# Sums over states in quads: batching the column-tiled matmuls of a selective scan

## Chip, cores, metric

One NeuronCore of a Trainium2 chip runs the whole kernel. The metric is the device time of one execution in microseconds; for the kernel before it is the median of three timed runs.

## The reference, cut to what matters

Two blocks run one after the other on x of (16, 192, 32, 32); each adds its result to x. The first is a convolution with a chunked state-space scan (SSD). The second is a selective scan:

```
proj  = seq @ W_proj.T + b_proj              # seq: (B, 1024, 192)
x_in, delta, Bm, Cm = split(proj)            # 192, 192, 16, 16 columns
delta = softplus(delta + dt_bias)
h_t = exp(delta_t * A) * h_{t-1} + (delta_t * x_t) * B_t      # (192 channels, 16 states)
y_t = sum over the 16 states of h_t * C_t    # the sums over states
out = (y + x_in * D) @ W_out.T + b_out
x   = x + out
```

Everything is float32.

## The kernel before

**Units.** The scan of one image is cut into two halves of 512 positions, and each half into 24 units. A unit is one block of 32 channels (`BLK`) with one group of 4 states, so that it fills 128 partitions. The first 16 units of a half (`WIDE`) are the four wide blocks, channels 0 to 127, group by group: units 4g to 4g + 3 are the four blocks of group g. The other 8 are the two narrow blocks, channels 128 to 191, two to a group. `unit(i)` gives group and block.

**The life of unit i.** ACT makes the decay exp(delta A) (L936), DVE the input product (L1220) and the scan over 512 positions (L1233, `hst`, a ring of 3). POOL multiplies by C into `hc`, a ring of 6 (`CRING`, L747). PE sums over the 4 states by a matmul with `sel` (128 x 32): the output are 32 partitions of the bank B_YSUM, at 32 times the block for wide units, so that the blocks of a group use different column tiles of the array. All groups of a half accumulate in the bank; `sum_states` opens it with diag1a times x_in. After the last wide sum ACT copies the bank (`copy_wide`, L942), PE opens the rows of the narrow blocks again (`start_rest`, diag1b), and after the last narrow sum ACT copies them (`copy_rest`).

**The batches.** `sum_states(n, k)` sums BATCH = 2 units, for whose products it waits by the semaphore hc_ready. PE raises y_sum_ps once a batch, and POOL waits for it before it writes the slot that held unit i - 6:

```
if i >= CRING or prev:
    pool.wait_ge(y_sum_ps.sem, y_sum_ps.at(n, (i - CRING) // BATCH + 1))
```

**The slots.** Every engine runs its own instructions in a fixed order that is written out by slots s = 0 to 47. One pass of 48 slots scans image b and does, woven in, the first block of image b + 1: fills (s = 0 to 2), four convolutions on PE (s = 3, 5, 7, 10) whose results ACT copies one slot later, eight chunks that start at s = 13, 15, ..., 27 and whose stages follow until s = 36, then the group means and variances of the result (s = 37, 38), and from s = 40 the projection of the second block. The output of the scan's first half (identity, wo1a and wo1b products, `finish`) is at s = 37 to 40, that of the second at s = 10 to 13 of the next pass. In slot s the scan is at unit s - 1 on DVE and at unit s - 2 on POOL. PE takes the batches at every even slot: units i, i + 1 (i even) at s = i + 4, first thing in the slot. The batches of units 44 to 47 fall into s = 0 and 2 of the next pass. There are 17 passes; 15 have both a scan and a first block, the one before them has no scan, the last no first block.

Line 1282 is that of the helper `mm`, which issues nearly all matmuls; L1366, L1380, L1381 and L1428 issue the rest. A float32 matmul is two instructions.

Of the kernel before, what the change touches and what calls it, by code (L numbers as in the profile page):

```python
# [49 lines left out]
NG = S1 // SG  # L50
NB = C // BLK
WB = P // BLK
HALF = L // 2
CPH = HALF // Q
HU = NG * NB
UNITS = 2 * HU
# [47 lines left out]
SLOTS_DU, DRING, WRING, HRING, CRING = 4, 3, 2, 3, 6  # L104
LEAD = 3


BATCH = 2
BATCHES = UNITS // BATCH
HALF_BATCHES = HU // BATCH  # L110
WIDE = NG * WB
WIDE_BATCHES = WIDE // BATCH


def unit(i):
# [56 lines left out]
def build(nc, scratch, x_d, inw_d, cw_d, cb_d, dtb_d, alog0_d, d0_d, nw_d, nb_d, outw_d,  # L172
          wp_d, bp_d, alog1_d, d1_d, dtb1_d, wo_d, bo_d, out_d):
    with ExitStack() as ctx:  # L174
# [209 lines left out]
        hc_ready = sig("hc_ready", UNITS)  # L384
        y_sum_ps = sig("y_sum_ps", BATCHES)
        y1_copied = sig("y1_copied", 4)
# [40 lines left out]
        for r in range(7):  # L427
            n = min(P, PROJ0 - r * P)
# [6 lines left out]
        for r in range(2):  # L435
            n = P if r == 0 else CB_
            for m in range(XM):
                jobs.append((nato[0:n, r, m * P:(m + 1) * P], n, P, [(wo0[:, m, r * P:r * P + n], 0, n)]))
        for r in range(4):
            n = min(P, PROJ1 - r * P)  # L440
# [10 lines left out]
        for r in range(2):  # L451
            n = P if r == 0 else CB_
# [196 lines left out]
        def _(pool):  # L649
# [86 lines left out]
            def states_by_c(n, i, prev):  # L736

                hf, (g, k) = i // HU, unit(i)
                pool.wait_ge(scanned.sem, scanned.at(n, i + 1))
                if k == 0:  # L740
                    pool.wait_ge(bc_read[g].sem, bc_read[g].at(n, 16 * (hf + 1)))
                if i == last_of_group(0, 0):

                    pool.wait_ge(kept_bc.sem, kept_bc.at(n, 16 * 4))
                if i >= CRING or prev:
                    pool.wait_ge(y_sum_ps.sem, y_sum_ps.at(n, (i - CRING) // BATCH + 1))  # L746
                nc.gpsimd.tensor_tensor(hc[:, i % CRING, :], hst[:, i % HRING, :], bcrep[:, g, 1, :],  # L747
                                        ALU.mult).then_inc(hc_ready.sem, 1)

# [18 lines left out]
        def _(act):  # L768
# [170 lines left out]
            def copy_wide(n, hf):  # L939

                act.wait_ge(y_sum_ps.sem, y_sum_ps.at(n, HALF_BATCHES * hf + WIDE_BATCHES))
                nc.scalar.copy(y1a[:, :], bank[B_YSUM][:, :]).then_inc(y1_copied.sem, 1)  # L942

            def copy_rest(n, hf):

                r = slice(hf * CB_, (hf + 1) * CB_)
                act.wait_ge(y_sum_ps.sem, y_sum_ps.at(n, HALF_BATCHES * (hf + 1)))
                nc.scalar.copy(y1b[r, :], bank[B_YSUM][r, :]).then_inc(y1_copied.sem, 1)
# [14 lines left out]
            def run(b, par, scan, end, first, more):  # L963
                step = Steps(act, act_steps, b + 1)
                mid_step = Steps(act, act_mid_steps, b)
                for s in range(SLOTS if scan or first else END_AT[1] + END_STEPS):
                    if scan:

                        decay(b, s, end, first)
                    if scan:  # L970
                        second_half(b, s, par, mid_step)
                    if first:
                        first_block(b + 1, s, step, 1 - par, scan, end)
                    if scan:
                        if 2 <= s < HU + 2:
                            act.wait_ge(scanned.sem, scanned.at(b, s - 1))
                            nc.scalar.copy(carry[:, s - 2:s - 1], hst[:, (s - 2) % HRING, HALF - 1:HALF]).then_inc(carried.sem, 1)  # L977
                        for hf in range(2):
                            if s == hf * HU + BATCH * WIDE_BATCHES + 2:
                                copy_wide(b, hf)  # L980
                        if s == HU + 2:
                            copy_rest(b, 0)
                    if end:
                        if s == 2:
                            copy_rest(b - 1, 1)
                        finish(b - 1, s, 1, 1 - par)
                    if scan:
                        finish(b, s, 0, par)
                assert not first or step.done == ACT_STEPS, step.done
# [281 lines left out]
        def _(pe):  # L1271
# [258 lines left out]
            def sum_states(n, k, prev):  # L1530

                hf, kk = k // HALF_BATCHES, k % HALF_BATCHES
                if kk == 0:
                    if hf or prev:
                        pe.wait_ge(y1_copied.sem, y1_copied.at(n, 2 * hf))
                    pe.wait_ge(p1_copied.sem, p1_copied.at(n, (K_XA, K_X2)[hf]))
                    mm(bank[B_YSUM][:, :], diag1a[:, :], xcm[:, PIECE[hf], :], True, False)
                pe.wait_ge(hc_ready.sem, hc_ready.at(n, BATCH * (k + 1)))
                for i in range(BATCH * k, BATCH * (k + 1)):
                    g, blk = unit(i)  # L1540
                    r0 = BLK * blk if blk < WB else hf * CB_ + BLK * (blk - WB)
                    ins = mm(bank[B_YSUM][r0:r0 + BLK, :], sel[:, :], hc[:, i % CRING, :], False, g == NG - 1)
                ins.then_inc(y_sum_ps.sem, 1)
# [20 lines left out]

            def run(b, par, scan, end, first, more):
                for s in range(SLOTS if scan or first else END_AT[1] + END_STEPS):
                    if s in (0, BATCH):
                        if end:
                            sum_states(b - 1, BATCHES - 2 + s // BATCH, False)
                    elif scan and s > 2 and (s - 2) % BATCH == 0:  # L1570
                        sum_states(b, (s - 2) // BATCH - 1, end)
                    for hf in range(2):
                        if scan and s == hf * HU + WIDE + 3:
                            start_rest(b, hf)
                    if end:
                        if scan and s == END_AT[1]:

                            pe.wait_ge(scanned.sem, scanned.at(b, 8))
                        if not scan and s == END_AT[1]:

                            pe.wait_ge(scanned.sem, scanned.at(b - 1, UNITS))
                        finish(b - 1, s, 1, 1 - par)
                        if s == SSD_AT + 5:

                            pe.wait_ge(out_ready.sem, out_ready.at(b - 1, 4))
                    if scan:
                        if first and s == END_AT[0]:

                            pe.wait_ge(row_exp.sem, row_exp.at(b + 1, NRB * NCH))
                        if s == END_AT[0]:  # L1590
                            pe.wait_ge(scanned.sem, scanned.at(b, 36))
                        finish(b, s, 0, par)
                    if first:
                        first_block(b + 1, s, end if scan else None)
                    if more and s == EARLY_AT + 1:
                        pe.wait_ge(p1_copied.sem, p1_copied.at(b + 1, 2))
                        group_means(b + 2, 0)
                    if more and s == EARLY_AT + 2:
                        group_variances(b + 2, 0)
# [47 lines left out]
```

## Time and profile before

| | |
|---|---|
| timed runs | 3646.38, 3640.47, 3628.37 us; median 3640.47 |
| the profiled execution | 3614.94 us, span 3613.2 us |
| mean granted TensorE clock | 0.929 |
| PE busy | 3140.8 us (87%) |
| weight loads (PEld) | 1812.4 us (50%) |
| DVE busy | 2674.8 us (74%) |
| ACT busy | 1840.2 us (51%) |
| POOL busy | 1507.1 us (42%) |
| POOL waits for DVE before L747 | 1143.3 us |
| PE waits for POOL's hc | 101.4 us |

A busy PE means that a matmul is in flight, not that the array is full. The granted clock is 1.00 at 2.4 GHz and 0.50 at 1.2 GHz. Times in rows are microseconds from the start of the span. In a timeline row stand the start, the duration, the engine and line, output and inputs, how many instructions are merged in it, and in brackets the idle time of the engine before it with what ended it.

### The profile page before, as it was taken

The page shows a single profiled execution, that of the slowest core. Times are in us where ns is not written, and L with a number is a line of the kernel's source. Part 1 is how long each engine was busy: PE and PEld are TensorE (multiplying, and loading weights), DVE is VectorE, ACT ScalarE, POOL GpSimd, SP SyncE. Part 2 cuts the span into 40 slices and gives each one's busy share as a digit, 9 for nine tenths or more (in the row PEclk, how much of TensorE's full clock was granted, in tenths as well). Part 3 has the DMA queues.
Part 4 walks back from the last instruction along what each step waited for, and adds up shares of the span by engine and source line. Part 5 has one row for each costly group of instructions (what it writes and reads, how often), then busy time and mean ns, then how long its engine had stood idle before and what let it go on. Part 6 is the DMA issues. An engine that isn't in the chain of part 4 may idle for free. (4 is left out here: it accounts for less than half of the span.)

```text
span 3613.2 us, 60645 instructions
## 1 busy us (share of the span) xinstructions
PE 3140.8 (87%) x20256; PEld 1812.4 (50%) x20256; DVE 2674.8 (74%) x3983; ACT 1840.2 (51%) x4315; POOL 1507.1 (42%) x1107
## 2 busy tenths in 40 slices
PE   4888889898899998889898898998899999888965
PEld 2655547364463735547364453735446364554710
DVE  1347877778677777878778787777868778787787
ACT  1536464554636446364553646446464554646432
POOL 1014444444444344444444444344434444444455
PEclk8999999998989989999998999999989998999976
DMA  2032141413214142141412314141231413214121
GB/s 58 14 103 64 39 137 36 132 68 93 85 45 123 56 123 71 38 134 38 131 68 85 91 44 131 50 131 68 70 101 45 117 68 105 79 47 133 36 99 65
DMA packets 104163, 290.96 MB, mean 81 GB/s; under 512 B 25373, under 2 KB 27020, under 8 KB 103820
## 3 DMA queue, kind: packets, MB, share of 16 engines
q1 hardware_dynamic: 103820, 286.71, 26.3%
q8 instruction: 176, 2.88, 0.3%
q14 instruction: 167, 1.37, 0.1%
HBM read 181.84 MB, written 39.85 MB: 61 GB/s over the span
## 5 line engine op out<-in xcount | busy, mean ns | idle before, releaser
L747 POOL TENSOR_TENSOR hc<-hst,bcrep 128x512 f32<-128x512 f32 x768 | 1202.5, 1566 | 1178.4 <-DVE hst L1233 1143.3
L833 ACT ACTIVATE ssd<-bank,ncs 128x128 f32<-128x128 f32 x1536 | 438.8, 384 | 237.2 <-PE bank L1282 237.0
L1282 PE MATMUL bank<-hc,sel 128*32 128x512 f32 x1536 | 454.3, 677 | 101.4 <-POOL hc L747 101.4
L1220 DVE TENSOR_TENSOR wr<-durep,bcrep 128x512 f32<-128x512 f32 x768 | 521.1, 679 | 3.6 <-DMA bcrep<-bc_rows 3.6
L1233 DVE TENSOR_TENSOR_SCAN hst<-dec,wr 128x512 f32<-128x512 f32 x256 | 392.4, 1533 | 92.5 <-ACT carry L977 58.5
L1282 PE MATMUL bank<-ssd 128*128 128x32 f32 (+1 forms) x3296 | 447.2, 288 | 0.0
L936 ACT ACTIVATE bank<-durep,aneg 128x512 f32<-128x512 f32 x368 | 253.9, 690 | 294.1 <-DVE hst L1233 285.5
L1282 PEld LDWEIGHTS bank<-ssd 128*128 128x128 f32 x3296 | 399.5, 193 | 4.2
L1282 PE MATMUL bank<-ssd,wcv 64*32 64x512 f32 x5376 | 349.7, 600 | 0.0
L1282 PE MATMUL bank<-xna,wt0a 128*128 128x128 f32 (+3 forms) x1088 | 296.1, 374 | 34.1 <-DVE xnb L1044 34.1
L866 ACT ACTIVATE ssd<-bank,nbc,nwc 128x128 f32<-128x128 f32 x384 | 147.5, 453 | 345.8 <-PE bank L1428 345.8
L1233 DVE TENSOR_TENSOR_SCAN hst<-bank,carry,wr 128x512 f32<-128x512 f32 x240 | 306.2, 1276 | 11.2 <-ACT bank L936 1.9
L936 ACT ACTIVATE dec<-durep,aneg 128x512 f32<-128x512 f32 x400 | 292.8, 738 | 6.7 <-DVE hst L1233 4.7
L714 POOL TENSOR_TENSOR lrs<-lve,neghalf 128x1 f32<-128x1 f32 x128 | 87.1, 680 | 484.4 <-DVE lve L1087 484.4
L1282 PE MATMUL bank<-xnb,wt0b 128*128 128x128 f32 (+3 forms) x1088 | 285.2, 364 | 0.0
L1081 DVE TENSOR_TENSOR ssd<-ssd,bank 128x384 f32<-128x384 f32 x112 | 62.1, 554 | 283.7 <-PE bank L1282 283.7
L1366 PE MATMUL bank<-ident,csum 128*128 128x128 f32 x1536 | 239.5, 280 | 17.7 <-ACT ssd L833 12.6
L708 POOL TENSOR_TENSOR ssd<-ssd,wend 128x384 f32<-128x384 f32 x112 | 144.0, 1286 | 248.6 <-ACT ssd L879 248.6
L1282 PE MATMUL bank<-ssd,wo 128*128 128x128 f32 (+1 forms) x1536 | 212.6, 280 | 33.4 <-DVE x1b L1112 33.3
L1282 PEld LDWEIGHTS bank<-xna,wt0a 128*128 128x128 f32 (+1 forms) x1088 | 174.2, 194 | 134.4 <-issue 86.4
L1099 DVE TENSOR_TENSOR ssd<-ssd,bank 128x1536 f32<-128x1536 f32 x128 | 223.4, 1746 | 23.1 <-ACT ssd L833 23.1
L1366 PEld LDWEIGHTS bank<-ident,csum 128*128 128x128 f32 x1536 | 184.6, 141 | 87.7 <-issue 41.7
(187 smaller groups left out, 5000.8 us busy)
## 6 DMA issues: line engine op xcount, KB each, us to landing
durep<-scratch SPq DMA_DIRECT2D x192, 512.0 KB, 3.7
bcrep<-bc_rows SPq DMA_DIRECT2D x128, 512.0 KB, 5.2
ssd<-stage SPq DMA_DIRECT2D x384, 140.4 KB, 2.9
ssd<-bcst SPq DMA_DIRECT2D x128, 74.4 KB, 2.7
xa<-in_x_dram SPq DMA_DIRECT2D x16, 512.0 KB, 4.0
scratch<-u SPq DMA_DIRECT2D x32, 256.0 KB, 2.1
scratch<-delta SPq DMA_DIRECT2D x32, 256.0 KB, 2.4
out_dram<-x1a SPq DMA_DIRECT2D x16, 512.0 KB, 4.8
```

Of the source, the lines that this page charges most:

```text
L708: nc.gpsimd.tensor_tensor(xw[:, c % 2, :].rearrange("p (h d) -> p h d", d=HD), xtok[:, c % 2, 0:DI].rearrange("p (h d) -> p h d", d=HD), b ...
L714: nc.gpsimd.tensor_tensor(lrs[:, c % 2:c % 2 + 1], lve[:, c % 2:c % 2 + 1], neghalf[:, 0:1], ALU.pow).then_inc(lrs_ready.sem, 1)
L747: nc.gpsimd.tensor_tensor(hc[:, i % CRING, :], hst[:, i % HRING, :], bcrep[:, g, 1, :], ALU.mult).then_inc(hc_ready.sem, 1)
L833: ins = nc.scalar.activation(att[:, c % 2, h, :], bank[ROW_BANKS[r]][:, k * Q:(k + 1) * Q], ACT.Exp, bias=ncs[:, c, h:h + 1])
L866: ins = nc.scalar.activation(yzt[:, c % 2, m, :], bank[B_CBT][:, (m + 1) * Q:(m + 2) * Q], ACT.Identity, bias=nbc[:, m:m + 1], scale=nwc[: ...
L936: nc.scalar.activation(decay_of(i), durep[:, j % SLOTS_DU, 0, :], ACT.Exp, scale=aneg1[:, g * NB + k:g * NB + k + 1]).then_inc(decay_ready ...
L1081: ins = nc.vector.tensor_tensor(y0[:, c % 2, :], yint[:, c % 2, :], bank[B_XY][:, 0:DI], ALU.add)
L1099: nc.vector.tensor_tensor(a, a, bc(bank[B_CBT][:, 0:Q].unsqueeze(1), [P, NH, Q]), ALU.mult).then_inc(att_ready.sem, 1)
L1220: nc.vector.tensor_tensor(wr[:, i % WRING, :], durep[:, j % SLOTS_DU, 1, :], bcrep[:, g, 0, :], ALU.mult).then_inc(w_made.sem, 1)
L1233: nc.vector.tensor_tensor_scan(hst[:, i % HRING, :], decay_of(i), wr[:, i % WRING, :], carry[:, g:g + 1] if hf else 0.0, ALU.mult, ALU.add ...
L1282: return nc.tensor.matmul(out, lhsT, rhs, start=start, stop=stop, skip_group_check=True)
L1366: nc.tensor.matmul(ps[:, k * Q:(k + 1) * Q], bc(csum[:, 0, c, h:h + 1], [P, P]), ident[:, :], start=(k == 0), stop=False, is_transpose=Tru ...
```

## The change

The wide units are now summed four at a time, which are the four blocks of a group, and the narrow ones two at a time as before. The quads stand at s = 6, 10, 14, 18 and s = 30, 34, 38, 42; there are 8 batches in a half instead of 12. A quad is due when its last unit is, which is where the second of its two pairs was; the first pair of each four moves there, two slots later. The product with diag1a moves with the first batch of a half, from s = 4 to 6 and from s = 28 to 30. POOL's wait for a ring slot counts the new batches. ACT's `copy_wide` stays at its slots.

```diff
-BATCH = 2
-BATCHES = UNITS // BATCH
-HALF_BATCHES = HU // BATCH
 WIDE = NG * WB
-WIDE_BATCHES = WIDE // BATCH
+BATCH_SIZES = (WB,) * NG + (NB - WB,) * NG
+HALF_BATCHES = len(BATCH_SIZES)
+BATCHES = 2 * HALF_BATCHES
+WIDE_BATCHES = NG
+BATCH_END = [hf * HU + sum(BATCH_SIZES[:k + 1]) for hf in range(2) for k in range(HALF_BATCHES)]
+
+
+def batch_of(i):
+
+    return min(k for k in range(BATCHES) if i < BATCH_END[k])
...
                 if i >= CRING or prev:
-                    pool.wait_ge(y_sum_ps.sem, y_sum_ps.at(n, (i - CRING) // BATCH + 1))
+                    pool.wait_ge(y_sum_ps.sem, y_sum_ps.at(n, batch_of(i - CRING) + 1 if i >= CRING else batch_of(i - CRING + UNITS) + 1 - BATCHES))
...
-                            if s == hf * HU + BATCH * WIDE_BATCHES + 2:
+                            if s == hf * HU + WIDE + 2:
                                 copy_wide(b, hf)
...
-                pe.wait_ge(hc_ready.sem, hc_ready.at(n, BATCH * (k + 1)))
-                for i in range(BATCH * k, BATCH * (k + 1)):
+                pe.wait_ge(hc_ready.sem, hc_ready.at(n, BATCH_END[k]))
+                for i in range(BATCH_END[k] - BATCH_SIZES[kk], BATCH_END[k]):
...
-                    if s in (0, BATCH):
-                        if end:
-                            sum_states(b - 1, BATCHES - 2 + s // BATCH, False)
-                    elif scan and s > 2 and (s - 2) % BATCH == 0:
-                        sum_states(b, (s - 2) // BATCH - 1, end)
+                    for k in range(BATCHES):
+                        if end and s + UNITS == BATCH_END[k] + 2:
+                            sum_states(b - 1, k, False)
+                        if scan and s == BATCH_END[k] + 2:
+                            sum_states(b, k, end)
```

## Rows read from the trace of the kernel before

**Rows 1.** the page, part 5: the sums over states (count, busy together, mean ns of one)
```profile
L1282 PE MATMUL bank<-hc,sel 128*32 128x512 f32 x1536 | 454.3, 677 | 101.4 <-POOL hc L747 101.4
```

**Rows 2.** busy times by pass, three of 14 and the sum; granted clock behind POOL
```profile
1320.40:1542.20 221.80, 198.83 (x1264) 114.96 (x1264) 166.46 (x248) 114.00 (x267) 93.19 (x68) 0.92 0.27 82
1542.20:1754.10 211.90, 190.51 (x1264) 110.13 (x1264) 165.69 (x248) 114.58 (x268) 90.64 (x67) 0.96 0.28 86
...
2610.40:2835.90 225.50, 203.42 (x1264) 117.01 (x1264) 165.70 (x248) 113.59 (x266) 92.34 (x68) 0.90 0.27 81
...
sum 3014.30, PE 2707.05 PEld 1571.47 DVE 2320.80 ACT 1597.03 POOL 1297.24; mean PE 193.36 PEld 112.25 DVE 165.77 ACT 114.07 POOL 92.66
```

**Rows 3.** timeline of PE, s = 28 to 33 (start, us, what; idle before)
```profile
1682.27 1.02 PE L1282 MATMUL bank<-xcm,diag1a 128*128 128x512 f32 x2
1683.23 1.05 PE L1282 MATMUL bank<-hc,sel 128*32 128x512 f32 x4
1684.21 0.91 PE L1282 MATMUL bank<-state,cs_ 128*128 128x384 f32 x2
...
1703.43 0.55 PE L1428 MATMUL bank<-ident,ssd 128*128 128x128 f32 x3 [0.82 <-DVE ssd L1091]
```

**Rows 4.** timeline of DVE, where it waits for PE
```profile
1509.59 0.16 DVE L1039 TENSOR_SCALAR gv<-bank 128x2 f32<-128x2 f32 x1 [4.08 <-PE bank L1282]
...
1689.08 0.55 DVE L1081 TENSOR_TENSOR ssd<-ssd,bank 128x384 f32<-128x384 f32 x1 [2.40 <-PE bank L1282]
...
1725.11 0.80 DVE L1044 TENSOR_SCALAR xnb<-x1b,gm,gr 64x1024 f32<-64x1024 f32 x1
...
1733.43 0.43 DVE L1049 TENSOR_SCALAR u<-ssd 128x512 f32<-128x512 f32 x1 [1.83 <-ACT ssd L913]
```

**Rows 5.** timeline of PE, s = 4 to 17
```profile
1568.35 1.13 PE L1282 MATMUL bank<-xcm,diag1a 128*128 128x512 f32 x2
...
1583.05 1.05 PE L1282 MATMUL bank<-hc,sel 128*32 128x512 f32 x4
1586.80 1.05 PE L1282 MATMUL bank<-hc,sel 128*32 128x512 f32 x4 [2.70 <-POOL hc L747]
...
1610.33 0.91 PE L1282 MATMUL bank<-state,cs_ 128*128 128x384 f32 x2 [2.11 <-DVE state L1059]
```

**Rows 6.** timeline of ACT before the last convolution's copies, in two passes
```profile
1375.11 0.68 ACT L796 ACTIVATE xs<-bank,cb 64x512 f32<-64x512 f32 x1 [2.72 <-PE bank L1282]
...
1594.44 0.68 ACT L796 ACTIVATE xs<-bank,cb 64x512 f32<-64x512 f32 x1 [1.07 <-PE bank L1282]
```

**Rows 7.** timeline of PE, a pair beside a projection onto 32 columns
```profile
1539.19 1.07 PE L1282 MATMUL bank<-hc,sel 128*32 128x512 f32 x2
1539.20 1.06 PE L1282 MATMUL bank<-xna,wt1a 128*32 128x512 f32 x1
```

**Rows 8.** timeline of PE, s = 37 to 40
```profile
1714.02 1.83 PE L1282 MATMUL bank<-x1a,ident 128*128 128x512 f32 x2
1716.22 0.38 PE L1282 MATMUL bank<-mv,ga 128*128 128x1 f32 x2 [0.38 <-DVE mv L1028]
...
1722.70 1.92 PE L1282 MATMUL bank<-hc,sel 128*32 128x512 f32 x4 [0.36 <-POOL hc L747]
...
1727.11 1.12 PE L1282 MATMUL bank<-xna,wt1a 128*128 128x512 f32 x2
```

**Rows 9.** granted clock (behind POOL) behind gaps of PE, in short stretches
```profile
1367.50:1370.50 3.00, 3.00 (x28) 1.18 (x34) 0.70 (x1) 2.97 (x8) 1.04 (x1) 0.50 0.00 0
...
1500.50:1514.00 13.50, 13.50 (x30) 5.03 (x31) 9.11 (x13) 1.96 (x3) 5.42 (x4) 0.50 0.37 126
1589.30:1592.30 3.00, 3.00 (x64) 1.09 (x56) 1.52 (x2) 2.97 (x8) 0.46 (x2) 1.00 0.02 5
...
3515.00:3570.00 55.00, 24.31 (x48) 2.85 (x48) 53.10 (x43) 17.84 (x35) 33.96 (x22) 0.50 0.30 100
```

**Rows 10.** timeline of PE in the last pass, one pair of many alike
```profile
3532.40 1.92 PE L1282 MATMUL bank<-hc,sel 128*32 128x512 f32 x4 [3.65 <-POOL hc L747]
```

## The prediction, made before the change was run

> **What bounds the kernel now.** I read the page first, then the busy times by pass, then one pass (1542.2 to 1754.1) engine by engine as a timeline, and last the stretches where the granted clock is low. A pass does a scan of one image (48 units of 512 positions, two halves of 24: 16 units of the wide blocks, then 8 of the narrow) and the first block of the next image, woven together by slots s = 0 to 47; 15 of the 17 passes do both. The sums over states are 1536 PE instructions, but they overlap: 454 us busy together for 1040 us of single durations [rows 1]. A pass takes 215.3 us in the mean over the 14 that I measured; the three shown take 211.9 to 225.5, and what differs between them is the clock: 0.96 in the shortest, 0.92 and 0.90 in the longer ones [rows 2]. So there are two kinds of limit: places where PE is the last to arrive, and places where PE is early but comes back from a gap at half clock.
>
> PE is the last to arrive in the chunk part (s = 20 to 31): it has nearly no gap, and DVE waits for it, 2.40 us before chunk 6 at 1689.08 [rows 3, 4]. After the last chunk DVE is the limit for most of the time, then PE's projection is (DVE waits 1.83 us at 1733.43 through ACT's softplus) [rows 4]. In s = 4 to 17 ACT and DVE set the time, with one exception: ACT waits 1.07 us for the last convolution, which PE began late because its sum at s = 10 waited 2.70 us for POOL [rows 5, 6].
>
> **The change part by part.** The order before is a pair at every even slot; after, the wide units have a quad at s = 6, 10, 14, 18 and at s = 30, 34, 38, 42. So the pairs at s = 4, 8, 12, 16, 28, 32, 36 and 40 go, the diag1a product that opens each half moves with its first batch (4 to 6, 28 to 30), and the pairs of the narrow units stay. No DMA is added or moved; instructions are as many as before.
>
> A quad's price: a pair takes 0.98 us from start to start (1683.23 to 1684.21) at full clock [rows 3]. No quad is in the trace. From above it can't cost more than two pairs, 1.96; from below not less than a pair. The nearest row is three column tiles at once: at 1539.19 two of hc and, 0.01 us later, one of the projection onto 32 columns start together, and take 1.07 and 1.06 us as tiles of a pair do at that clock [rows 7]. I take 0.98 for a quad. The Trainium skill (TensorE: Matmul & The Clock Gate, Measured speedup vs the span model) gives 3.07 times for four row tiles, not 4; by that a quad would be near 1.1 us, and 8 quads would give back about 1 us a pass if all lay on the path.
>
> *s = 28 and 30.* Before: diag1a 0.96 + pair 0.98 at s = 28, pair 0.98 at s = 30. After: nothing, then 0.96 + 0.98. The first chunk output comes 1.94 earlier, which DVE's wait of 2.40 allows; by the next, net gain 1.94 - 0.96 = 0.98. With up to 0.15 for a dearer quad I take 0.88. PE is gap-free in between, so it goes to the end of the pass.
>
> *s = 40.* In the pass shown PE waits 0.36 for POOL, then the pair takes 1.92 at half clock (from 1722.70), and the projection starts at 1727.11. It needs DVE's xnb, done at 1725.91 (1725.11 + 0.80) [rows 4, 8]. Without the pair PE is there first, so the gain is 1727.11 - 1725.91 = 1.2 us, and DVE's wait of 1.83 leaves room for it. Bounds: 0 and 1.83.
>
> *s = 32, 36.* The next PE work waits for DVE: 0.82 us at 1703.43 and 0.38 at 1716.22 [rows 3, 8]. No gain. *s = 4, 8, 12, 16.* At 4 and 8 PE is ahead (2.70 of gap follows), at 12 ACT is the limit, at 16 the gap of 2.11 at 1610.33 follows [rows 5]. No gain.
>
> Gain, with the clock as it is: 15 passes x (0.88 + 1.2) = 31 us.
>
> *What the empty places cost.* The hidden pairs were what kept PE's gaps short.
> First, s = 7 to 10. The convolution now ends 1.94 - 0.96 = 0.98 earlier and the pair at 1583.05 is gone, while the sum at s = 10 still waits for unit 7 at 1586.80, which hangs on DVE and ACT. The gap of 2.70 becomes 1586.80 - 1582.07 = 4.7 us. Behind it are quad, identity product and the convolution for which ACT waits. What a low clock costs there is in the trace: in the pass from 1320.4 the clock was at its lower level, 1.2 GHz (0.50 from 1367.5 on), after the same gap of 2.70, and ACT waited 2.72 instead of 1.07 us: 1.65 us [rows 6, 9]. In the pass from 1542.2 it stayed at 1.00. Low after this gap: 4 of the 14 passes, counted in the same way. The last pass shows what longer gaps do: with 3.65 us between pairs PE ran at 0.50 for all of 3515 to 3570 [rows 9, 10]. I take it that after 4.7 us it is always low, and for longer (up to 3.3, two such stretches; nothing if it stays high): 2.2 us in about 10 passes more, 22 us.
> The Trainium skill (same page, HAM oscillation) says that idle PE between bursts drops the clock each time; if so, all passes pay here, and the trace agrees for gaps of 3.65 us, while after 2.70 it goes both ways.
> Second, s = 17: the gap of 2.11 [rows 5] becomes 3.1, before from_state and chunk 0, for which DVE waits. Low there in 3 of 14 passes; I take half: 5 more x 1.65 = 8 us (0 to 20).
> Third, s = 36 to 38. The identity product (1714.02) follows a pair that took 1.9 us at half clock; without it, it starts at 1712.1 and at full clock ends by 1713.1; then nothing until 1716.22 [rows 8]: a gap of 3.1 us. Behind it lie the group sums, the quad, four output products and the group variance, which DVE needs. In the pass from 1320.4 the clock was 0.50 from 1500.5 to 1514.0, and DVE waited 4.08 us for the variance (1509.59); in the pass from 1542.2 not at all [rows 4, 9]. Long low stretches are in 5 of 14 passes. I take 12 of 15: 7 more x 4.1 = 29 us (0 to 41).
>
> Sum: -31 + 22 + 8 + 29 = +28 us. The profiled execution took 3614.94 us (span 3613.2), so 3643 in its terms. The three timed runs have a median of 3640.47, 25.5 above it; the profile's own passes differ by up to 13.6 us (225.5 - 211.9) through the clock, so I read these 25 us as more passes with a low clock. A part of the loss is then already in the median. I count 12 of the 28 instead: 3652.
>
> **The rivals.**
> A, *the clock stays as it was.* The gaps grow but the clock falls no more often than now; only the 31 us remain: 3640 - 31 = 3609. For it: after 2.70 us the clock stayed up in 10 of 14 passes, and total PE work is no less dense. Against: 4.7 us is longer than any gap in these 14 passes. It decides if the clock is at 1.00 behind the sum at s = 10 in more than half of the passes.
> B, *the forecast*: gains eaten by half-clock stretches, 3652.
> C, *heavier*: the low stretch behind s = 10 lasts over the whole convolution (3.3 us a pass) and the one at s = 36 comes in every pass: 15 x (2.1 - 3.3 - 1.65 x 0.5) + the third at 41 gives about 71 of loss less what is paid already (25): 3686.
> D, *the four tiles don't run together*: a quad costs 1.96. Then s = 28 and 30 gain 0, s = 40 keeps its 18 us, and the gaps still cost 59: 3640 + 41, less the 16 already paid: 3665. Against it: three tiles at once in the trace.
> E, *POOL waits for its ring.* hc has 6 slots, and units 4m and 4m + 1 come free two slots later than before. POOL needs them two slots behind the quad. If each wait lasted a quad: 8 x 0.98 x 16 = 125 us, 3765. Against: the pairs before were four slots ahead, and half of that is left.
>
> **How the numbers follow.** A 0.30, B 0.48, C 0.14, D 0.05, E 0.03. B's own range is 3635 to 3675. The range over all that holds 8 in 10 goes from A's 3605 to 3686. A change of 0.5% (18 us) is about what a measurement can tell from none: faster means under 3622, slower over 3659. Faster: A and a trace of B, 0.31. Same: most of B, 0.35. Slower: the rest of B with C, D, E, 0.34.
>
> **What would show it.** A quad's eight instructions spanning about 1.05 us at full clock (D wrong). Chunks 5 to 6 closer by about 2 us, 6 to 7 farther by about 1 us. PE idle 4.7 us before the sum at s = 10 and the clock 0.50 behind it; ACT's wait for the last convolution over 2.7 us. DVE's wait of about 4 us for the variance in most passes. Mean clock down from 0.929 to about 0.90. A mean clock of 0.93 or more would make B wrong and A right; POOL waits for PE above today's would speak for E.

## The result: 0.7% slower

After, five runs: 3661.28 to 3669.55 us, median 3666.45. Before, in five runs beside them: 3628.37 to 3646.38, median 3642.82. The ratio after to before is 1.0068, 95% interval 1.0045 to 1.0091. So the change costs about 24 us, more than the 0.5% that can be told from none. In the later comparisons, with 16 to 27 runs, the kernel before had medians of 3627 to 3634 and single runs from 3596 to 3661: its time varies from run to run more than that of the kernel after, whose five runs lie within 8.3 us.

The profiled execution after took 3669.55 us (span 3667.8), mean granted clock 0.904. Before it was 3614.94 (3613.2) and 0.929. The profiles are thus 54.6 us apart where the medians are 24: the profiled run of before was one of its quick ones. Where the time went is read from the profiles, how much it is from the medians.

The page of the kernel after, part 1 (busy time of PE to POOL) and the group of part 5 that stands in [rows 1]:
```profile
PE 3101.3 (85%) x20256; PEld 1839.3 (50%) x20256; DVE 2677.0 (73%) x3983; ACT 1841.4 (50%) x4315; POOL 1519.0 (41%) x1107
...
L1288 PE MATMUL bank<-hc,sel 128*32 128x512 f32 x1536 | 317.0, 713 | 135.1 <-POOL hc L753 135.1
```
The change did what it says. The same 1536 instructions are busy together for 317 us instead of 454, and PE for 3101 instead of 3141. DVE, ACT and POOL have the same work. The mean of one sum rose from 677 to 713 ns, although nothing in it changed: 366 of the 1536 now start in a stretch at half clock, before 252. (Lines from L753 on stand 6 further down than before.)

Busy times by pass of the kernel after, as in [rows 2] (granted clock behind POOL), three of 14 and their sum:
```profile
1339.00:1560.60 221.60, 194.17 (x1266) 115.51 (x1264) 166.61 (x248) 113.99 (x267) 93.91 (x68) 0.91 0.27 82
1560.60:1779.30 218.70, 191.71 (x1264) 114.47 (x1264) 165.92 (x248) 114.37 (x268) 91.67 (x67) 0.91 0.27 82
...
2656.50:2878.20 221.70, 194.21 (x1264) 115.40 (x1264) 165.98 (x249) 113.99 (x268) 94.39 (x68) 0.91 0.27 82
...
sum 3067.30, PE 2679.16 PEld 1596.45 DVE 2323.18 ACT 1597.64 POOL 1309.56; mean PE 191.37 PEld 114.03 DVE 165.94 ACT 114.12 POOL 93.54
```
A pass takes 219.1 us (3067.3 / 14) instead of 215.3. Before, 7 of the 14 took 209.3 to 211.9 and the others up to 225.5. Now all but the first take 218.2 to 221.7, at a clock of 0.91 to 0.92: the quick passes are gone, and so are the slowest.

To find the place I cut each pass at events of DVE and ACT that stand in the same order in both kernels, and took the mean over the 14 passes of each trace. The cuts: DVE's first write of xna (start), ACT's last copy of a convolution, DVE's first statistics instruction (lst) behind the outputs of chunks 0, 1, 5, 6 and 7, its read of the group variance (gv), its product u of delta and x. Worked out from starts in the traces, us:

```
                 conv.  chunk 0  0-1    1-5    5-6    6-7    gv     u      end   pass
before           55.69  19.54   11.96  49.03  13.46   9.42  23.83  19.40  12.97  215.3
after            57.41  20.84   12.89  49.03  11.42  10.48  24.16  19.74  13.13  219.1
difference       +1.72  +1.30   +0.93   0     -2.04  +1.06  +0.33  +0.34  +0.16   +3.8
```
Times 14 (unrounded) this is 53.1; what stands ahead of the 14 passes is 5.1 longer and what stands behind them 3.6 shorter, which makes the 54.6 by which the spans differ.

**The places themselves.** Timeline of PE after, s = 6 to 18 and 36 to 37, in the pass that is the counterpart of [rows 5]:
```profile
1592.36 1.13 PE L1288 MATMUL bank<-xcm,diag1a 128*128 128x512 f32 x2
1593.41 1.06 PE L1288 MATMUL bank<-hc,sel 128*32 128x512 f32 x8
1594.41 0.46 PE L1288 MATMUL bank<-da,upper 128*128 128x96 f32 x2
...
1605.20 1.94 PE L1288 MATMUL bank<-hc,sel 128*32 128x512 f32 x8 [4.65 <-POOL hc L753]
1607.07 2.08 PE L1288 MATMUL bank<-x1a,ident 128*128 128x512 f32 x2
...
1631.39 1.65 PE L1288 MATMUL bank<-state,cs_ 128*128 128x384 f32 x2 [3.09 <-DVE state L1065]
...
1644.41 1.13 PE L1288 MATMUL bank<-state,cs_ 128*128 128x384 f32 x2 [2.96 <-DVE state L1068]
...
1733.81 1.74 PE L1288 MATMUL bank<-ssd,wo 128*128 128x128 f32 x12 [1.06 <-DVE x1b L1118]
1736.96 1.13 PE L1288 MATMUL bank<-x1a,ident 128*128 128x512 f32 x2 [1.41 <-DVE hst L1239]
1739.56 0.38 PE L1288 MATMUL bank<-mv,ga 128*128 128x1 f32 x2 [1.47 <-DVE mv L1034]
```
A quad costs 1.00 us from start to start (1593.41 to 1594.41) at full clock and 1.87 at half (1605.20 to 1607.07). The first two gaps are the ones that the forecast worked out: 4.7 and 3.1 us. The one of 2.96 us behind them was as long before. The forecast's third gap, 3.1 us ahead of the group sums (mv,ga), is not there: the identity product waits for DVE's scan and splits it into 1.41 and 1.47 us.

Who waits behind them, ACT and DVE in the same pass ([rows 4, 6]):
```profile
1615.51 0.68 ACT L802 ACTIVATE xs<-bank,cb 64x512 f32<-64x512 f32 x1 [3.74 <-PE bank L1288]
```
```profile
1637.85 0.56 DVE L1084 COPY ssd<-bank 128x384 f32<-128x384 f32 x1 [4.22 <-PE bank L1288]
1650.90 0.55 DVE L1087 TENSOR_TENSOR ssd<-ssd,bank 128x384 f32<-128x384 f32 x1 [4.07 <-PE bank L1288]
...
1699.93 0.56 DVE L1087 TENSOR_TENSOR ssd<-ssd,bank 128x384 f32<-128x384 f32 x1 [2.77 <-PE bank L1288]
1711.35 0.56 DVE L1087 TENSOR_TENSOR ssd<-ssd,bank 128x384 f32<-128x384 f32 x1 [0.35 <-PE bank L1288]
1721.84 0.56 DVE L1087 TENSOR_TENSOR ssd<-ssd,bank 128x384 f32<-128x384 f32 x1 [2.26 <-PE bank L1288]
...
1735.62 1.28 DVE L1239 TENSOR_TENSOR_SCAN hst<-bank,carry,wr 128x512 f32<-128x512 f32 x1
...
1746.33 0.16 DVE L1045 TENSOR_SCALAR gv<-bank 128x2 f32<-128x2 f32 x1 [1.46 <-PE bank L1288]
```
ACT waits 3.74 us where it waited 1.07 (or 2.72 in the pass with a low clock there). Before chunk 6 DVE's wait of 2.40 has shrunk to 0.35: the gain at s = 28 is there.

Busy times in short stretches of that pass, granted clock behind POOL, as in [rows 9]:
```profile
1604.00:1607.00 3.00, 1.80 (x8) 0.20 (x8) 2.72 (x3) 2.92 (x6) 1.84 (x2) 0.50 0.00 0
1607.00:1610.00 3.00, 3.00 (x16) 1.40 (x20) 0.82 (x1) 2.99 (x7) 0.93 (x1) 0.50 0.00 0
...
1631.50:1634.50 3.00, 3.00 (x9) 2.13 (x10) 2.11 (x3) 0.14 (x1) 1.63 (x1) 0.50 0.21 81
1645.00:1648.00 3.00, 3.00 (x14) 2.52 (x12) 1.83 (x3) 1.14 (x4) 1.49 (x1) 0.50 0.00 0
...
1740.50:1743.80 3.30, 3.30 (x11) 0.72 (x11) 3.09 (x7) 0.00 (x0) 1.63 (x1) 0.50 0.80 264
1743.90:1747.20 3.30, 3.30 (x13) 1.45 (x12) 1.73 (x4) 1.27 (x2) 2.26 (x2) 1.00 0.48 150
1747.30:1754.00 6.70, 6.65 (x8) 1.75 (x8) 6.61 (x8) 2.07 (x3) 3.18 (x2) 0.50 0.01 6
```
A low stretch is a stretch of time at half clock. In 14 of 14 passes one begins behind s = 10 (before in 4), in 13 and 13 behind the gaps ahead of the first two products with a state (before in 3 and 5), which the outputs of chunks 0 and 1 follow. The third stretch stands at s = 37 to 40, and the last three rows show it from s = 38 on: it is broken up, low behind the gap, high, low again into the projection at s = 40.

### The profile page after: what moved, and what is told of

Same layout as the page of the kernel before. It is cut to its first block and busy times, and to the rows that moved or that the text cites. A ratio compares the mean times of both kernels' runs of the same rounds, so it can differ in the third digit from the quotient of the medians.

```text
span 3667.8 us, 60519 instructions
## 1 busy us (share of the span) xinstructions
PE 3101.3 (85%) x20256; PEld 1839.3 (50%) x20256; DVE 2677.0 (73%) x3983; ACT 1841.4 (50%) x4315; POOL 1519.0 (41%) x1107
## 5 line engine op out<-in xcount | busy, mean ns | idle before, releaser
L753 POOL TENSOR_TENSOR hc<-hst,bcrep 128x512 f32<-128x512 f32 x768 | 1213.8, 1581 | 1205.0 <-DVE hst L1239 1154.5
L1288 PE MATMUL bank<-hc,sel 128*32 128x512 f32 x1536 | 317.0, 713 | 135.1 <-POOL hc L753 135.1
L1372 PE MATMUL bank<-ident,csum 128*128 128x128 f32 x1536 | 250.0, 289 | 32.5 <-ACT ssd L839 26.4
L1372 PEld LDWEIGHTS bank<-ident,csum 128*128 128x128 f32 x1536 | 193.2, 146 | 108.0 <-issue 50.1
L1288 PE MATMUL bank<-ssd,wo 128*128 128x128 f32 (+1 forms) x1536 | 212.3, 281 | 26.3 <-DVE x1b L1118 26.3
```

Of the source, the lines that this page charges most:

```text
L1288: return nc.tensor.matmul(out, lhsT, rhs, start=start, stop=stop, skip_group_check=True)
L1372: nc.tensor.matmul(ps[:, k * Q:(k + 1) * Q], bc(csum[:, 0, c, h:h + 1], [P, P]), ident[:, :], start=(k == 0), stop=False, is_transpose=Tru ...
```

## The experiments

"Dummy pairs" are products with a tile of zeros, added to the open bank, so that the result doesn't change; each pair is four instructions, as dear as a pair of hc. The edit is the same in all kernels that have them, and only the table differs:

```diff
+            def keep_busy(s):
+                where, pairs = KEEP_BUSY.get(s, (None, 0))
+                for _ in range(pairs):
+                    for r0 in (0, BLK):
+                        mm(bank[where][r0:r0 + BLK, :], nosel[:, :], wt0a[:, 0:HALF], where != B_YSUM, where != B_YSUM)
...
+                    if scan and first and s != 18:
+                        keep_busy(s)
```
At s = 18 they go to another bank, since ACT reads the sums then. The last pass has none. Theory 1 is the forecast's: PE's idle time, and the half clock behind it, is the cost of the change.

**First set: parts of the change, and less work.** Beside these four the kernel before had a median of 3634.01.

*e1_fill_back*, from the kernel after:
```diff
+KEEP_BUSY = {8: (2, 2), 16: (2, 1), 36: (2, 1)}
```


> Changed kernel plus dummy products (zero weights, 128 x 32, added to the open bank, so nothing changes in the result) in the places of the removed pairs ahead of PE's gaps: two pairs at s = 8, one at s = 16, one at s = 36. PE's gaps are then about as long as before the change, and nothing else differs from the changed kernel. Theory (the clock falls behind longer gaps): the gain of 31 us shows, 3600 to 3630 us; clock 0.92 or more. Rival (the quads or POOL's ring waits cost the time): adding 4 pairs of work a pass can't help, 3666 us or more. Rival (the clock falls whatever one does): 3660 to 3670.

Measured: 3664.14, ratio 1.0087 (1.0053 to 1.0122), in the range of the last rival and not of the theory.

*e2_quads_first_half* and *e3_quads_second_half* have quads in one half of the image only:
```diff
-BATCH_SIZES = (WB,) * NG + (NB - WB,) * NG
+SIZES = ((WB,) * NG + (NB - WB,) * NG, (2,) * (HU // 2))     # e2
+SIZES = ((2,) * (HU // 2), (WB,) * NG + (NB - WB,) * NG)     # e3
```


> Quads in the first half only (s = 6 to 18), pairs in the second half. Theory: this part has the costs (gaps before the sums at s = 10 and before s = 17) and no gain: 3665 to 3700 us, slower than both. Rival (quads cost by themselves, evenly): half of the change's 24 us, about 3655.

> Quads in the second half only (s = 30 to 42), pairs in the first. Theory: this part has both gains (0.9 us at s = 28 and 30, 1.2 us at s = 40, in 15 passes) and only the third gap: 3600 to 3630 us, faster than before. Rival (quads cost by themselves): about 3655.

Measured: e2 3722.28, ratio 1.0248 (1.0208 to 1.0289); e3 3667.57, ratio 1.0101 (1.0067 to 1.0134).

*e4_less_work* is the kernel before with pairs everywhere, where the sums of units 4, 5, 12 and 13 of the first half take only the first of their 512 columns (this part of the sums is left out):
```diff
+                    w = 1 if i in THIN else HALF
-                    ins = mm(bank[B_YSUM][r0:r0 + BLK, :], sel[:, :], hc[:, i % CRING, :], False, g == NG - 1)
+                    ins = mm(bank[B_YSUM][r0:r0 + BLK, 0:w], sel[:, :], hc[:, i % CRING, 0:w], False, g == NG - 1)
```


> Kernel before, but the pairs of units 4, 5 (s = 8) and 12, 13 (s = 16) sum only 1 of their 512 columns; that part of the sum is left out. PE does nearly 2 us of work less a pass, and no wait or order changes. Theory: the gaps before s = 10 and s = 17 grow to 3.6 and 3.0 us, the clock falls behind them more often, and the kernel is slower with less work: 3655 to 3690 us. Rival (a pair in PE's idle time costs nothing, leaving it out changes nothing): 3635 to 3648.

Measured: 3733.83, ratio 1.0268 (1.0228 to 1.0308), clock 0.898. PE timeline of this kernel, the rows with a gap at the three places:
```profile
1624.80 1.92 PE L1288 MATMUL bank<-hc,sel 128*32 128x512 f32 x4 [3.55 <-POOL hc L753]
...
1651.01 1.65 PE L1288 MATMUL bank<-state,cs_ 128*128 128x384 f32 x2 [2.92 <-DVE state L1065]
1664.02 1.13 PE L1288 MATMUL bank<-state,cs_ 128*128 128x384 f32 x2 [2.97 <-DVE state L1068]
```
This is the clearest run of the four. Two pairs all but gone in front of two gaps, nothing moved and no quad, and the kernel is 100 us slower, far beyond what was expected. The clock is low at the same three places as in the kernel after (14, 13 and 14 of 14 passes). About half of the 8.8 us a pass falls at the third stretch (gv and u in the table below, 2.8 and 1.8), whose gaps the edit doesn't touch: the clock is low there for 13.6 to 20.5 us in all 14 passes, before in 5. The run speaks against any theory in which the quads' order or their price is the cost.

The other three missed too: e2 is 22 us over the upper end of what was expected, and e1 and e3, expected at 3600 to 3630, are as slow as the kernel after. With the same cuts as above:

```
                 conv.  chunk 0  0-1    1-5    5-6    6-7    gv     u      end   pass
e1 fill back     55.48  20.06   13.47  49.75  11.42  10.49  24.73  20.51  12.51  218.4
e2 first half    57.66  20.65   13.02  49.03  13.45   9.41  25.38  19.76  12.57  220.9
e3 second half   56.00  19.91   13.33  49.66  11.42  10.49  24.70  20.56  12.87  218.9
e4 less work     57.57  20.70   13.02  49.04  13.46   9.42  26.62  21.15  13.14  224.1
```
Quads in the second half alone bring the gain between chunks 5 and 7 and leave the gap at s = 10 as it was (2.73 us), though the clock is low behind it in 7 passes instead of 4. But there the clock is low for longer ahead of chunk 1, behind a gap that is the same in all these kernels (12 passes of 14, before 5), and in the third stretch in all passes. The halves aren't additive either: 5.6 and 3.6 us a pass alone, 3.8 together. So a part of the change moves low stretches to gaps that it leaves alone. Theory 1 had to say what happens when no gap is left.

**Second set: fill more.** The kernel before had a median of 3627.21 here.

*e5_dummy_pairs_at_old_places*, from the kernel after, a pair at each place that lost one but s = 4 and 28:
```diff
+KEEP_BUSY = {8: (2, 1), 12: (2, 1), 16: (2, 1), 32: (2, 1), 36: (2, 1), 40: (2, 1)}
```


> The kernel after, with a dummy pair (four products of a zero weight tile, 128x32 by 128x512 each, as dear as a pair of hc) behind s = 8, 12, 16, 32, 36 and 40, where the kernel before has pairs; only s = 4 and 28 stay without. Results are not changed by it, PE's work is more than before's. Theory 1 (PE's idle time and the clock that follows from it make the loss): every gap is as long as in the kernel before, so the time is before's less the gain at s = 28 and 30, 15 x 0.95 = 14 us: 3610 to 3640, ratio to before 0.993 to 1.001. Rival (the quads themselves, by the order in which hc and the bank come free, or dummy work that delays PE): no better than the kernel after, 3660 or more.

Measured: 3656.99, ratio 1.0091 (1.0056 to 1.0126): a miss. PE timeline at s = 8 to 10:
```profile
1585.44 1.05 PE L1290 MATMUL bank<-wt0a,nosel 128*32 128x512 f32 x4
1590.17 1.94 PE L1290 MATMUL bank<-hc,sel 128*32 128x512 f32 x8 [3.68 <-POOL hc L755]
```
The expectation said that every gap is as long as before. It isn't: the convolution still ends 0.98 us earlier, because the pair of s = 4 isn't there, and the gap is 2.70 + 0.98 = 3.68. The clock is low behind it in all 14 passes, and the first cut is at 58.75. The third stretch, with the old pairs back at s = 32, 36 and 40, is near that of before (24.26 and 18.94).

*e6_one_quad*, only units 24 to 27 as a quad at s = 30:
```diff
+SIZES = ((2,) * (HU // 2), (WB,) + (2,) * 10)
```


> Only units 24 to 27 are summed as a quad, at s = 30; all other units go in pairs as before. So only the pair at s = 28 is gone, with its diag1a product moved to s = 30. Theory 1: the gain of 0.95 us a pass at s = 28 and 30 is there and no gap grows, 3640 - 14 = 3620 to 3630, ratio 0.996. Rival (the clock hits passes by their position, and any shift of a microsecond decides in how many of them a stretch goes low): anything from 3610 to 3670, with the low stretches of before in other passes.

Measured: 3638.5, ratio 1.003 (0.9997 to 1.0064), no difference that can be told from none. The 0.97 us gain between chunks 5 and 7 is there (11.42 + 10.49 against 13.46 + 9.42), and it is lost: low behind the unchanged gap ahead of chunk 1 in 10 passes instead of 5, gv 24.77 instead of 23.83. The rival, that any shift of a pass changes where the clock falls, fits better than theory 1 here.

*e7_before_filled*, the kernel before (pairs in both halves), with its own gaps filled, and *e8_after_filled*, the kernel after with all gaps over a microsecond filled but those at the pass's seam:
```diff
+KEEP_BUSY = {8: (2, 2), 16: (2, 1), 18: (0, 2), 35: (2, 1), 37: (2, 1)}                                  # e7
+KEEP_BUSY = {8: (2, 4), 16: (2, 2), 18: (0, 2), 32: (2, 1), 35: (2, 1), 36: (2, 2), 40: (2, 1)}      # e8
```


> The kernel before with dummy pairs of zero weights in its own gaps: two behind s = 8, one at s = 16, two at s = 18, one at s = 35 and one at s = 37; results are not changed. Theory 1: the gaps of 2.70, 2.11, 2.96 and those around s = 36 fall under 1.5 us, so the low stretches at 46, 70, 84 and 180 us of a pass come less often; with none of them all passes take the 211.5 of the fast ones or less, 16 x 3.8 = 60 us under the mean of after and 15 x 2 to 4 under this kernel's median: 3580 to 3615. Rival (filling moves the low stretches but doesn't take them away, as in the first experiment; the dummy pairs cost where they overlap with real work): 3630 to 3670.

> The kernel after with dummy pairs in all its gaps of over a microsecond: four behind s = 8, two at s = 16, two at s = 18, one at s = 32 and s = 35, two at s = 36, one at s = 40; results are not changed. Theory 1: no gap over 1.5 us is left but that at a pass's start, the low stretches at 43, 70, 84 and 180 us of a pass vanish, and each of their costs as measured in the trace of after (2.7, 2.1, 1.6 and 1.0 us) comes back, with the gain at s = 28 and 30 on top: a pass of 211 or less, 3570 to 3610. Rival (some of the low stretches stay, at other places): 3620 to 3670. If the dummy work only delays: over 3670.

Measured: e7 3579.04, ratio 0.9879 (0.9838 to 0.9920); e8 3563.38, ratio 0.9824 (0.9786 to 0.9863). Both are faster than both kernels, by doing more work; e7 is 1 us and e8 7 us under the lower end of what was expected. PE timeline of e8, s = 8 to 10 in one pass, then s = 18 in another:
```profile
1779.64 3.63 PE L1290 MATMUL bank<-wt0a,nosel 128*32 128x512 f32 x16
1784.38 1.06 PE L1290 MATMUL bank<-hc,sel 128*32 128x512 f32 x8 [1.11 <-POOL hc L755]
...
1786.55 5.38 PE L1290 MATMUL bank<-ssd,wcv 64*32 64x512 f32 x96
```
```profile
1601.26 1.89 PE L1290 MATMUL bank<-wt0a,nosel 128*32 128x512 f32 x8
1604.32 0.91 PE L1290 MATMUL bank<-state,cs_ 128*128 128x384 f32 x2 [1.17 <-DVE state L1070]
```
Busy times of e8 at the former low stretches (granted clock behind POOL), and its page:
```profile
1562.00:1582.00 20.00, 18.84 (x190) 5.33 (x174) 15.74 (x16) 18.62 (x32) 11.27 (x7) 1.00 0.00 1
1590.00:1610.00 20.00, 17.58 (x124) 12.45 (x120) 14.60 (x23) 9.10 (x30) 8.46 (x7) 1.00 0.33 108
1690.00:1705.00 15.00, 13.05 (x66) 5.27 (x60) 14.56 (x26) 4.17 (x7) 9.36 (x8) 1.00 0.31 106
1705.00:1718.00 13.00, 11.18 (x30) 3.10 (x31) 12.02 (x16) 6.81 (x12) 6.20 (x4) 1.00 0.05 21
```
```profile
L1290 PE MATMUL bank<-hc,sel 128*32 128x512 f32 x1536 | 292.2, 643 | 85.2 <-POOL hc L755 85.2
```
What waits still waits as long (PE's real work comes at the same time), but it finds the clock at 1.00. From the second of the 14 passes on there is no low stretch between 35 and 198 us of a pass. The same quads now take 643 ns each, not 713.

e8 is 16 us under e7 (not compared with each other in one ratio; both against the same runs of before). I had expected this from the gain of 0.97 us a pass at s = 28. The passes don't bear that out: they take 212.7 and 212.8, because e8 gives the gain back at the seam, where its convolutions end later (57.81 against 56.07): the clock is low in the first 40 us of a pass for 10.5 us in the mean, in e7 for 6.6. In the profiles e8 is 9.1 shorter, 8.3 of it in the last pass.

**Third set: one group of gaps opened again.** Each kernel is e8 without some of its dummy pairs. The kernel before had a median of 3632.6.
```diff
+KEEP_BUSY = {16: (2, 2), 18: (0, 2), 32: (2, 1), 35: (2, 1), 36: (2, 2), 40: (2, 1)}               # e9
+KEEP_BUSY = {8: (2, 4), 32: (2, 1), 35: (2, 1), 36: (2, 2), 40: (2, 1)}                            # e10
+KEEP_BUSY = {8: (2, 4), 16: (2, 2), 18: (0, 2)}                                                    # e11
+KEEP_BUSY = {44: (2, 2), 47: (2, 2), 8: (2, 4), 16: (2, 2), 18: (0, 2), 32: (2, 1), 35: (2, 1), 36: (2, 2), 40: (2, 1)}   # e12
```
In e12 those of s = 44 and 47 go to the rows of the narrow blocks, which are open then, and at s = 44 they stand behind the slot's projection.

> The kernel after with all the dummy pairs of the eighth experiment but the four behind s = 8, so that the gap of about 4.7 us before the quad at s = 10 is open again. Theory 1 (a gap brings half clock behind it and that is the cost, each gap for itself): the clock is 0.50 for about 7 us behind s = 10 in nearly every pass and the last convolution comes 2.7 us later, 15 x 2.7 = 40 us: 3595 to 3610 beside 3563. Rival (the costs aren't separate: the low stretch shifts the pass against the others, and what was filled stays filled, or later gaps get shorter by it): under 3580 if the delay is absorbed, over 3625 if other stretches fall too.

> The same without the dummy pairs at s = 16 and s = 18, so that the gaps of about 3.1 and 3.0 us before the first two state products are open. Theory 1: low stretches of 3.4 us at 70 and 84 us of a pass in most passes, for which DVE waits: 2.1 + 1.6 us a pass as in the trace of after, 15 x 3.7 = 55 us: 3600 to 3625. Rival: these gaps go low only when the one at s = 10 has gone low before (in the kernel before they fell in few passes); then under 3580.

> The same without the dummy pairs at s = 32, 35, 36 and 40. Theory 1, with the size as measured in after: low stretches around 180 us of a pass, 1.0 us a pass to the group variance and 1 more to the end by the projection at half clock: 3575 to 3600. With the size of the forecast, 4.1 us a pass: 3620 to 3630.

> All the dummy pairs of the eighth experiment and two more pairs at s = 44, ahead of the second group variance of the image after next (gap of 2.5 us), and two at s = 47, ahead of the next pass's first product (gap of 2.0 to 4.7 us). Results are not changed. Theory 1: the low stretches at 0 to 24 us of a pass (10 to 17 us in most passes) get rarer; before that the first products of a pass came up to 3.5 us later than in passes without: 3520 to 3560. Rival (what follows there waits for DVE or for loads, or the many products of 12 columns bring the low clock by themselves): 3560 to 3570, or over 3570 if the pairs delay the projection.

Measured: e9 3607.46, ratio 0.9925 (0.9892 to 0.9958); e10 3618.01, 0.9963 (0.9933 to 0.9992); e11 3614.39, 0.9963 (0.9932 to 0.9994); e12 3557.7, 0.9776 (0.9733 to 0.9819).

The rows that decide, of e9, e10 and e11: the instruction behind the gap in the timeline (in e11 DVE's read of the variance), and the granted clock of the stretch:
```profile
1576.48 1.93 PE L1290 MATMUL bank<-hc,sel 128*32 128x512 f32 x8 [4.67 <-POOL hc L755]
...
1575.60:1582.30 6.70, 5.82 (x33) 1.85 (x41) 4.29 (x4) 6.60 (x12) 2.98 (x3) 0.51 0.00 0
1590.00:1640.00 50.00, 45.06 (x297) 31.39 (x298) 39.23 (x57) 30.46 (x93) 21.63 (x18) 1.00 0.25 80
```
```profile
1812.34 1.65 PE L1290 MATMUL bank<-state,cs_ 128*128 128x384 f32 x2 [3.09 <-DVE state L1067]
...
1811.40:1825.00 13.60, 12.66 (x51) 11.19 (x52) 6.37 (x13) 3.26 (x12) 3.32 (x4) 0.50 0.37 129
```
```profile
1929.10 0.16 DVE L1047 TENSOR_SCALAR gv<-bank 128x2 f32<-128x2 f32 x1 [4.25 <-PE bank L1290]
...
1919.50:1939.50 20.00, 19.91 (x40) 7.10 (x41) 14.97 (x19) 3.81 (x6) 9.45 (x7) 0.50 0.25 88
```
```
                 conv.  chunk 0  0-1    1-5    5-6    6-7    gv     u      end   pass
e7 before filled 56.07  19.23   11.91  49.15  13.46   9.42  22.37  18.90  12.31  212.8
e8 after filled  57.81  19.23   11.32  49.04  11.42  10.49  22.56  18.51  12.30  212.7
e9 first open    59.24  19.19   11.32  49.04  11.42  10.49  23.76  18.83  12.26  215.5
e10 second open  56.55  21.52   12.24  49.03  11.42  10.48  23.01  18.70  12.14  215.1
e11 third open   55.02  19.23   11.32  49.04  11.42  10.49  25.80  20.58  12.83  215.7
e12 seam filled  58.00  19.23   11.32  49.04  11.42  10.49  22.55  18.28  11.88  212.2
```
Opening one group costs 44, 55 and 51 us by the medians, or 37, 50 and 50 by the differences of the ratios to before (x 3630), where theory 1 had said 40, 55 and 12 to 37. For e11 the size of the forecast (3620 to 3630) was nearer. Each open gap brings its low stretch back at its own place: behind s = 10 in 14 passes in e9, behind the two gaps ahead of the state products in 12 and 8 in e10, in the third stretch in 14 in e11. e11 has no gap over 1.8 us at the third stretch (1.80, 1.69, 1.41 and 1.47 in most passes). There a low stretch of up to 20 us from s = 37 on makes DVE wait 4.25 us for the variance; the stages gv and u cost 5.3 us more than in e8 (25.80 + 20.58 against 22.56 + 18.51), and 2.8 of it come back in the next pass's first stage. The separation isn't perfect. The third stretch, filled in e9 and e10 just as in e8, is low for a few us in 12 and 11 passes, which adds 1.2 and 0.45 us a pass at gv. And the three costs sum to 150 us (137 by the ratios), while the kernel after is 103 above e8 (3666.45 against 3563.38, in different comparisons), so they don't add here either.

e12 is the fastest kernel of the study, 2.2% under the kernel before and (3557.7 / 3666.45) 3.0% under the one after, at a clock of 0.954. Filling the seam brought 6 us by the medians, 17 by the ratios, whose intervals overlap (0.9733 to 0.9819 against 0.9786 to 0.9863): the late stretch behind 198 us of a pass is gone, but the start of the pass, with the many products of 12 columns, is still low for 10 us in the mean.

## Why the forecast came out, and which of its terms didn't

The forecast was 3652 with 3605 to 3686 around it; the time was 3666. That is on B's side (3635 to 3675), but past the 3659 over which I had called it slower, with a chance of 0.34. Rival A, the clock as it was (3609), is out: the mean clock is 0.904, not 0.93. Of C, the low stretch at s = 37 comes in every pass, but it is short, and in the pass shown ACT's wait for the last convolution grew by 2.67 (3.74 against 1.07), not by 3.3. Of B's terms, in us over the 14 passes of the table above beside the forecast's 15:

- **Price of a quad**: 0.98 taken, 1.00 measured. D is wrong. The Trainium skill (TensorE: Matmul & The Clock Gate, Measured speedup vs the span model) gives 3.07 times for four row tiles and has no row for four column tiles. I had put a quad near 1.1 by it, which doesn't follow: from the 0.96 of a single product (diag1a) the estimate by that figure is 4 x 0.96 / 3.07 = 1.25. Four column tiles of float32 do better here, four sums in the time that two took plus 2%.
- **s = 28 and 30**: chunk 6 is 2.04 us earlier, chunk 7 then 1.06 later, net 0.98 a pass, 14 us. Right, as is the picture (2 closer, 1 farther).
- **s = 40**: forecast -18, measured +5 (19.74 against 19.40 from gv to u). The pair went, but the projection that should have profited begins at half clock in every pass (before in 1). With the clock up (e8) this stage is 18.51, with it down (e11) 20.58. The term was counted at the clock of the quickest passes.
- **First gap**: 4.7 forecast, 4.65 measured, low in all 14 passes, as said. Forecast 22, measured 24 (1.72 a pass in the mean).
- **Second gap**: this term of the sum was sized too small: forecast 8, measured 31 (1.30 + 0.93 a pass). The gap of 3.09 is what was forecast, but the clock is low behind it in 13 passes and not in half, and the gap of 2.96 behind it, which the change doesn't touch and which I had left out, is low in 13 instead of 5. e10 gives 55 us for the two together.
- **Third gap**: this step of the forecast was wrong; forecast 29, measured 5. I had let the identity product start as soon as the pair ahead of it was gone (1712.1) and got a gap of 3.1 us. But it waits for DVE's scan, which ends at 1736.90 in the pass shown, and starts at 1736.96. So the idle time is 1.41 and 1.47 us, and the long gap never came. The clock is low behind it all the same, in all 14 passes. The price of a long low stretch was right (DVE's wait for the variance in e11 is 4.25; 4.08 in [rows 4]), but in 12 of 14 passes the stretch is broken up (3.4 and 6.8 us with a high piece between), not 13.6 to 20.5 us long as in the 5 bad passes of before. DVE's wait is 1.46 in the pass shown, where I had named about 4 in most passes as a sign. In these 12 the stage gv takes 23.9 us, between the 22.4 of the 9 passes of before without a long low stretch there and the 26.3 to 26.7 of its 5 bad ones, and so about what the mean was before (23.83).
- **Sum**: forecast +28 against the profiled time, measured +54.6. The two mis-sized terms on one side (second gap 23 short, s = 40 23 short) are only partly offset by the third (24 too much). That the time came within 14 us of the forecast is thus in part luck.
- **From the profile to the median**: I took 12 of the 28, because before's median lies above its profiled run by its low passes. This held in kind: 54.6 in the profiles became 24 in the medians. In the terms of the profile the forecast was 3643, and the profiled run took 3669.55.
- **E** is not what happened. POOL's waits for PE are below. They are above the 31.7 us in 20 waits of before, which I had named as a sign for E, but two of the 15 are of 13.1 us, in the last of the 14 passes and in the one behind it; the other 13 sum to 19.8. And e8 has the same quads and 46.5 us of these waits, and is 103 us faster.

The list of waits of the kernel after (sum in us, times, longest):
```profile
POOL hc L753 <- PE bank L1288: 46.0, 15, 13.1
```

So the mechanism is shown: a gap in PE's work brings half clock to the work behind it, others wait for that work, and the hidden pairs had kept those gaps short. e4 shows it with no quad at all, e8 by its reverse, e9 to e11 place by place. Not settled is what decides whether the clock falls behind a gap of 2.1 to 3.0 us. It did in some passes and not in others that look alike in PE's rows, and shifts of a microsecond upstream changed the count (e1, e3, e6). That is why no single part of the change has a cost of its own that could be added to the others', and why e1, e2, e3 and e5 all missed. Why e2 costs more than the whole change is in the table in part: against the kernel after it lacks the gain between chunks 5 and 7 (1.0 us a pass), and its third stretch is long in 10 of 14 passes (gv 25.38 against 24.16). Its median is another 27 above its profiled run (3695.64), and that stays open.

## What to carry to other kernels

Before you make hidden work on PE cheaper, look at what follows the gap that it leaves: if the next PE work is one that others wait for, price it at half clock. Where PE waits for other engines ahead of such work, products with a zero tile are worth trying, in all gaps at once: 1 to 2% here, with 420 to 780 instructions more and nothing else changed. A part of the change tested alone may say little when the clock reacts to all gaps together; leave-one-out from a version with every gap filled did tell the parts apart.

## What the hardware showed that I had not expected

- Less work made the kernel slower by 2.7% (e4): four sums of 32 partitions shortened in the first half of each image.
- A gap's effect on the clock, by passes: behind s = 10 it was low after 2.70 us in 4 of 14 passes (before), after 2.84 in 6 (e1), and after 3.55, 3.68 and 4.65 in all 14 (e4, e5, after); and with the gap filled to 1.1 us in none (e8). Behind the gap of 2.96 ahead of chunk 1, the same length in each, it was low in 5 (before), 13 (after), 12 (e3) and 10 passes (e6).
- Short gaps in a row can do it too: at the third stretch no gap of the kernel after is over 1.8 us, and the clock fell there in all 14 passes. With dummy pairs in them, and none over 1.2 us left, it fell only in the first (e8).
- A low stretch came without a gap too: in the timeline of the kernel after PE has no idle time from 1739.56 on (group means, quad, output products, group variances of one column each, output products), the clock is 1.00 from 1743.9, and it falls to 0.50 at 1747.3 for the next 6.7 us, in which the projection begins.
- Four column tiles at once take 1.00 us for float32 over 512 columns, two 0.98.
